# Perceiver block on one core: the first key group ahead of the queries, its loads first, GpSimd's fill of ones behind the norm

## The chip, the cores and the metric

One core of one Trainium2 chip. The metric is the device time of one execution in microseconds (us). The kernel before takes 1380.67 us, the median of three runs.

## The reference, cut to what matters

The program runs six residual layers over x (256 tokens, 256 features). The change lies in the first, a cross-attention of x to a context of 4096 tokens with 16 heads of 16 features:

```python
x = x + _L0_xattn_ref(_layernorm(x), ctx_1024, ctx_1024, Wq, bq, Wk, bk, ...)

Q = _linear(query, Wq, bq)      # 256 x 256, by heads
K = _linear(key, Wk, bk)        # 4096 x 256, by heads
V = _linear(value, Wv, bv)
scores = einsum('bhqd,bhkd->bhqk', Q, K) / sqrt(16)
# mean, maximum and variance of the softmax of scores give a temperature t for each head
attn = softmax(qk / (2 t))
out = _linear(attn @ V, Wo, bo)
```

The other five layers (linear attention, a block with 32 experts, a second cross-attention, multi-query attention, a mixture of 8 experts) are the same before and after.

## The kernel before, in words

The layer is `cross0`. It has several blocks, one after the other, and at the end of each block all engines meet at a barrier. The change touches only the first block, which computes the queries and the keys and splits both into three bfloat16 parts each (value, rest, rest of the rest), so that later float32 score products can be made from bfloat16 matmuls.

*VectorE* takes the layer norm of x (`layer_norm`, L118 to L129: statistics, `_rstd` at L124, a root on ScalarE, then xn at L128) and signals `xn_ready`. It then waits for the query matmuls, adds the bias (L342), signals `q_read`, splits the queries (L345 to L348), signals `q_split`, and sums them (L350). Then come the eight key groups, three instructions each (L355, L358, L360, the last signals `split_done`).

*TensorE* transposes xn (L158), multiplies it by wq (L291), and then makes eight key groups (L304). A group is one quarter of the context (1024 tokens, `ctxT`) by one half of the features: groups 0 to 3 are the four quarters with the first half, 4 to 7 the same with the second half. Four PSUM buffers hold the groups in turn. The transposes use buffer 0, the query product buffer 1, and group n uses buffer (n + 2) mod 4.

*ScalarE* takes the root, copies the transposed xn to SBUF (`xnT`, L318) and evacuates each group twice, as float32 (`whole`, L327) and as the first bfloat16 part (`parts`, L329). `whole` has two buffers, `parts` four. So group n waits for the split of group n - 2, and from group 4 on for the store of group n - 4:

```python
act.wait_ge(s["projected"], n + 1)
if n >= 2:
    act.wait_ge(s["split_done"], n - 1)
if n >= 4:
    act.wait_ge(stored[n % 4], 16 * (n // 4))
```

*SyncE* issues every DMA, in the order of the code. These are x, the identity, wq, bq, wk, the key bias `bcol`, and the four quarters of the context (L246 to L253). Then it waits for `q_split`, stores the three query parts (L257), waits for their landing, reads them back in another layout in six DMAs (L115), loads eight pieces of later weights (L263 to L268), and only then takes up the key groups: it waits for `split_done` of group n and stores its parts (L273). After group 3 it waits for all four stores and loads the keys of head 0 and 1 (L106), then stores groups 4 to 7.

*GpSimd* fills three rows of `k96` with ones (L311).

The next block (scores, from L450) starts at the barrier.

## Time and profile before

| | us |
|---|---|
| median of 3 runs | 1380.67 |
| lowest and highest run | 1380.11, 1383.14 |
| the profiled execution, its own time | 1385.94 |
| its span in the profile | 1384.2 |
| end of the first block's last split in that span | 49.33 |

The span is cut off a little at both ends of the execution, so it is 1.7 us shorter than the execution's own time. Times in the rows are in microseconds from the span's start. PE is TensorE, PEld its weight loads, DVE VectorE, ACT ScalarE, POOL GpSimd, SPq the queue of DMA issues on SyncE. A float32 matmul leaves two records in the trace, so four key matmuls of a half group (two blocks of 512 columns, two halves of the contraction) leave eight. Matmul records overlap; the rate is read from how many fall in a stretch, not from the length of one. What stands behind "<-" in brackets is what ended the idle time, as inferred by the view.

### The profile page before, as it was taken

What the parts mean: (1) busy time and instruction counts of PE and PEld (TensorE: products, weight loads), DVE (VectorE), ACT (ScalarE), POOL (GpSimd) and SP (SyncE); (2) the same over time, 40 slices, a digit from 0 to 9 for tenths busy, and PEclk for the clock granted to TensorE, in tenths of its full rate; (3) what the DMA queues carried; (4) which work ended last, traced back from release to release, by engine and by line L of the source; (5) the groups of instructions that cost most, each with busy time, mean ns of one, the idle gap of its engine ahead of it and who ended that gap; (6) DMA issues with size and microseconds to landing.
All of it is one profiled execution on the core that took longest, in us unless ns stands there. A gap on an engine that the chain in (4) does not pass through costs nothing. (4 is left out here: it accounts for less than half of the span.)

```text
span 1384.2 us, 25745 instructions
## 1 busy us (share of the span) xinstructions
PE 1129.8 (82%) x8423; PEld 694.0 (50%) x8423; DVE 816.0 (59%) x1508; ACT 899.7 (65%) x1208; POOL 630.7 (46%) x293
## 2 busy tenths in 40 slices
PE   7687877858999958979987788888888888857798
PEld 3343443433443436668872444454444444434687
DVE  6688888871111175552225787888887787735312
ACT  3599999967989724523322788888888888535110
POOL 2277777750000005000001899999999999800000
PEclk9799999988999968989995899999999999968899
DMA  7875445537555061004457899999999999524140
GB/s 253 249 220 129 119 118 134 125 91 149 106 118 99 0 208 64 1 31 152 152 214 247 309 324 313 312 327 331 323 316 325 313 330 324 189 70 168 45 138 8
DMA packets 97048, 257.51 MB, mean 186 GB/s; under 512 B 11193, under 2 KB 41305, under 8 KB 85466
## 3 DMA queue, kind: packets, MB, share of 16 engines
q1 hardware_dynamic: 96992, 256.79, 59.6%
q8 instruction: 32, 0.52, 0.2%
q14 instruction: 24, 0.20, 0.0%
HBM read 165.31 MB, written 91.92 MB: 186 GB/s over the span
## 5 line engine op out<-in xcount | busy, mean ns | idle before, releaser
L1916 POOL TENSOR_TENSOR xb_row<-xb_row,w_mask 128x1024 f32<-128x1024 f32 x128 | 419.4, 3293 | 246.3 <-DVE xb_row L1946 246.0
L1946 DVE TENSOR_TENSOR xb_row<-xb_cont_ps,xb_row 128x1024 f32<-128x1024 f32 x128 | 156.7, 1224 | 89.6 <-PE xb_cont_ps L1747 86.6
L554 DVE TENSOR_REDUCE xa_stats<-xa_b_ps 128x1 f32<-128x1024 f32 x128 | 155.7, 1219 | 33.4 <-PE xa_b_ps L470 32.8
L1784 PE MATMUL xb_turn_ps<-_ident,xb_row 128*128 128x128 f32 x1024 | 142.5, 284 | 38.8 <-ACT xb_row L1869 29.0
L1957 DVE CUSTOM_DVE_ANT_0 xb_row<-xb_row,xb_minus 128x1024 f32<-128x1024 f32 x128 | 165.5, 1293 | 0.0
L1784 PEld LDWEIGHTS xb_turn_ps<-_ident,xb_row 128*128 128x128 f32 x1024 | 113.6, 144 | 95.9 <-issue 61.2
L1747 PE MATMUL xb_cont_ps<-xb_kk,xb_qq 32*128 32x512 f32 x528 | 157.1, 673 | 2.4 <-DVE xb_row L1946 1.3
L1875 ACT COPY xb_turned<-xb_turn_ps 128x1024 f32<-128x1024 f32 x128 | 129.6, 1012 | 41.1 <-PE xb_turn_ps L1784 40.6
L1869 ACT ACTIVATE xb_row<-xb_row,xb_ntop 128x2048 f32<-128x2048 f32 x64 | 128.2, 2003 | 42.2 <-DVE xb_ntop L1963 42.2
L864 ACT ACTIVATE xa_probs<-xa_psT,xa_t_now 128x1024 f32<-128x1024 f32 x128 | 141.2, 1114 | 20.6 <-PE xa_psT L823 20.4
L1747 PE MATMUL xb_rel_ps<-xb_kk,xb_qq 32*128 32x512 f32 x496 | 145.9, 666 | 5.2 <-ACT xb_out L1864 4.0
L522 ACT ACTIVATE xa_exps<-xa_b_ps,xa_stats 128x1024 f32<-128x1024 f32 x128 | 141.2, 1108 | 13.5 <-DVE xa_stats L554 13.4
L1864 ACT COPY xb_out<-xb_rel_ps 128x1024 f32<-128x1024 f32 x124 | 124.8, 1006 | 29.8 <-PE xb_rel_ps L1747 16.1
L629 POOL TENSOR_TENSOR xa_rest<-xa_exps 128x1024 f32<-128x1024 f32 x48 | 90.9, 1894 | 99.9 <-ACT xa_exps L522 99.9
L1797 PE MATMUL xb_sum_ps<-xb_turned,xb_vhead 128*17 128x128 f32 x2048 | 82.5, 280 | 33.3 <-ACT xb_turned L1875 33.0
L1404 POOL TENSOR_TENSOR b_tc<-b_raw,w_waves 128x512 f32<-128x512 f32 x4 | 5.1, 1269 | 227.5 <-ACT b_raw L1390 227.5
L470 PE MATMUL xa_b_ps<-xa_k,xa_q 96*128 96x512 bf16 x256 | 71.0, 390 | 27.9 <-ACT xa_exps L522 17.3
L532 ACT ACTIVATE xa_squares<-xa_exps 128x1024 f32<-128x1024 f32 x80 | 84.2, 1053 | 0.5
L491 PE MATMUL xa_b_ps<-xa_wv,xa_ctxT 128*128 x512 | 67.2, 286 | 18.1 <-ACT xa_exps L522 18.1
L796 PE MATMUL xa_sums<-xa_probs,xa_vhead 128*17 128x256 f32 x1024 | 80.8, 389 | 0.2 <-ACT xa_probs L864 0.2
L491 PEld LDWEIGHTS xa_b_ps<-xa_wv,xa_ctxT 128*128 128x128 f32 x512 | 61.7, 196 | 33.1 <-ACT xa_exps L522 29.6
L1797 PEld LDWEIGHTS xb_sum_ps<-xb_turned,xb_vhead 128*17 128x17 f32 x2048 | 45.5, 98 | 63.4 <-ACT xb_turned L1875 51.9
(364 smaller groups left out, 1824.4 us busy)
## 6 DMA issues: line engine op xcount, KB each, us to landing
xb_row<-rel_scores SPq DMA_DIRECT2D x128, 512.0 KB, 5.9
rel_scores<-xb_out SPq DMA_DIRECT2D x32, 1024.5 KB, 5.7
rel_scores<-xb_out SPq DMA_DIRECT2D x32, 1024.0 KB, 5.3
b_e_w<-in_L_ffn_e_w SPq DMA_DIRECT2D x32, 513.0 KB, 3.5
w_w<-in_L_ffn_w SPq DMA_DIRECT2D x24, 512.0 KB, 4.6
xa_k<-first_parts SPq DMA_DIRECT2D x24, 384.0 KB, 5.1
value_rows<-xa_values SPq DMA_DIRECT2D x16, 544.0 KB, 6.1
xb_kk<-key_blocks SPq DMA_DIRECT2D x17, 512.0 KB, 7.8
```

The costliest lines, as they stand in the source:

```text
L491: mm = nc.tensor.matmul(out[:, n * P:(n + 1) * P], ctxT[:, k, at:at + P], wv[:, bass.ds(it, 1), k, :], start=(k == 0), stop=(k == KC - 1))
L522: nc.scalar.activation(exps[:, u % 4], ps[:, slot % 4], ACT.Exp, scale=-1.0, bias=stats[:, c % 2, 0, u:u + 1], accum_out=stats[:, c % 2, 1 ...
L554: nc.vector.tensor_reduce(stats[:, c % 2, 0, u:u + 1], ps[:, slot % 4], AX, ALU.min).then_inc(s["min_ready"], 1)
L864: nc.scalar.activation(probs[:, g % 4].rearrange("p c n -> p (c n)"), ps[:, g % 2], ACT.Exp, scale=t_now[:, b:b + 1]).then_inc(probs_ready, 1)
L1747: mm = nc.tensor.matmul(out[:, k * BANK:(k + 1) * BANK], qq[rows, b, kind, t * P:(t + 1) * P], kk[rows, b, half], start=True, stop=True)
L1784: mm = nc.tensor.transpose(turn_ps[:, k * P:(k + 1) * P], row[:, u, at:at + P], f.ident[:])
L1797: mm = nc.tensor.matmul(sum_ps[at:at + DV, 0:P], vhead[:, b, half * NCH // 2 + part * CPS + k, :], turned[:, part, k, :], start=(part == 0 ...
L1869: nc.scalar.activation(row[:, u], row[:, u], ACT.Exp, bias=ntop[:, u:u + 1]).then_inc(s["exp_done"], 1)
L1875: nc.scalar.copy(turned[:, part].rearrange("p k n -> p (k n)"), turn_ps[:]).then_inc(turned_sb[part], 1)
L1916: nc.gpsimd.tensor_tensor(row[:, u, at:at + SUB], row[:, u, at:at + SUB], mask[:, t, half * HALF + at:half * HALF + at + SUB], ALU.mult).t ...
L1946: nc.vector.tensor_tensor(row[:, u, at:at + SUB], cont_ps[:], row[:, u, at:at + SUB], ALU.add).then_inc(s["cont_out"], 1)
L1957: nc.vector.tensor_tensor_reduce(out=row[:, u, at:at + SUB], in0=row[:, u, at:at + SUB], in1=minus[:, t, half * HALF + at:half * HALF + at ...
```

## The change

Four edits, all in the first block:

1. SyncE issues wk third and the first quarter of the context fourth. bcol, wq and bq come behind them, ahead of the second quarter.
2. TensorE makes key group 0 first, then the transposes, group 1, the query matmuls, and groups 2 to 7. It waits for `q_read` ahead of group 3 instead of group 2, since the query product and group 3 share PSUM buffer 1.
3. ScalarE evacuates group 0 before it copies xnT. VectorE splits group 0 (`split_keys(0)`) before the queries (`split_queries`). SyncE's code behind the loads stays as it is.
4. GpSimd waits for `xn_ready` before it fills the ones.

```diff
--- before.py
+++ after.py
@@ -245,11 +245,12 @@
             def _(sp):
                 sp.dma_start(f.x[:], i["x"].rearrange("b (t p) d -> p (b t) d", p=P)).then_inc(s["x_loaded"], 16)
                 sp.dma_start(f.ident[:], i["c_ident"]).then_inc(s["x_loaded"], 16)
-                sp.dma_start(wq[:], rows_of(i["L0_xattn_Wq"])).then_inc(s["q_w_loaded"], 16)
-                sp.dma_start(bq[:], i["L0_xattn_bq"]).then_inc(s["q_w_loaded"], 16)
                 sp.dma_start(wk[:, 0], rows_of(i["L0_xattn_Wk"])).then_inc(s["k_w_loaded"], 16)
-                sp.dma_start(bcol[:, 0], i["L0_xattn_bk"]).then_inc(s["k_w_loaded"], 16)
                 for g in range(NQU):
+                    if g == 1:
+                        sp.dma_start(bcol[:, 0], i["L0_xattn_bk"]).then_inc(s["k_w_loaded"], 16)
+                        sp.dma_start(wq[:], rows_of(i["L0_xattn_Wq"])).then_inc(s["q_w_loaded"], 16)
+                        sp.dma_start(bq[:], i["L0_xattn_bq"]).then_inc(s["q_w_loaded"], 16)
                     sp.dma_start(ctxT[:, :, g * QUARTER:(g + 1) * QUARTER],
                                  rows_of(i["ctx_1024"])[:, :, g * QUARTER:(g + 1) * QUARTER]).then_inc(ctx_loaded[g], 16)
                 sp.wait_ge(s["q_split"], 1)
@@ -280,21 +281,10 @@
 
             @block.tensor
             def _(pe):
-                pe.wait_ge(s["x_loaded"], 32)
-                pe.wait_ge(s["xn_ready"], 1)
-                flat = ps[:, 0, 0:KC * S].rearrange("p (c n) -> p c n", c=KC)
-                transpose_tokens(nc, flat, xn, f.ident[:]).then_inc(s["xnT_mm"], 1)
-                pe.wait_ge(s["q_w_loaded"], 32)
-                pe.wait_ge(s["xnT_sb"], 1)
-                for m in range(KC):
-                    for c in range(KC):
-                        mm = nc.tensor.matmul(ps[:, 1, m * S:(m + 1) * S], wq[:, c, m * P:(m + 1) * P], xnT[:, c, :],
-                                              start=(c == 0), stop=(c == KC - 1))
-                mm.then_inc(s["q_mm"], 1)
-                pe.wait_ge(s["k_w_loaded"], 32)
-                for n, (g, t) in enumerate(key_groups):
+                def group(n):
+                    g, t = key_groups[n]
                     pe.wait_ge(ctx_loaded[g], 16)
-                    if n == 2:
+                    if n == 3:
                         pe.wait_ge(s["q_read"], 1)
                     if n >= 4:
                         pe.wait_ge(s["evacuated"], n - 3)
@@ -306,18 +296,38 @@
                                                   start=(c == 0), stop=(c == KC - 1))
                     mm.then_inc(s["projected"], 1)
 
+                pe.wait_ge(s["k_w_loaded"], 16)
+                group(0)
+                pe.wait_ge(s["x_loaded"], 32)
+                pe.wait_ge(s["xn_ready"], 1)
+                flat = ps[:, 0, 0:KC * S].rearrange("p (c n) -> p c n", c=KC)
+                transpose_tokens(nc, flat, xn, f.ident[:]).then_inc(s["xnT_mm"], 1)
+                group(1)
+                pe.wait_ge(s["q_w_loaded"], 32)
+                pe.wait_ge(s["xnT_sb"], 1)
+                for m in range(KC):
+                    for c in range(KC):
+                        mm = nc.tensor.matmul(ps[:, 1, m * S:(m + 1) * S], wq[:, c, m * P:(m + 1) * P], xnT[:, c, :],
+                                              start=(c == 0), stop=(c == KC - 1))
+                mm.then_inc(s["q_mm"], 1)
+                for n in range(2, len(key_groups)):
+                    group(n)
+
             @block.gpsimd
             def _(pool):
+                pool.wait_ge(s["xn_ready"], 1)
                 nc.gpsimd.memset(k96[ROWS:MAXROWS], 1.0).then_inc(s["ones_set"], 1)
                 pool.wait_ge(s["ones_set"], 1)
 
             @block.scalar
             def _(act):
                 take_root(f, act, s["var_ready"], s["root_ready"])
-                act.wait_ge(s["xnT_mm"], 1)
-                nc.scalar.copy(xnT[:], ps[:, 0, 0:KC * S].rearrange("p (c n) -> p c n", c=KC)).then_inc(s["xnT_sb"], 1)
                 act.wait_ge(s["k_w_loaded"], 32)
                 for n, (g, t) in enumerate(key_groups):
+                    if n == 1:
+                        act.wait_ge(s["xnT_mm"], 1)
+                        nc.scalar.copy(xnT[:], ps[:, 0, 0:KC * S].rearrange("p (c n) -> p c n", c=KC)
+                                       ).then_inc(s["xnT_sb"], 1)
                     act.wait_ge(s["projected"], n + 1)
                     if n >= 2:
                         act.wait_ge(s["split_done"], n - 1)
@@ -336,19 +346,7 @@
                 dve.wait_ge(s["x_loaded"], 32)
                 layer_norm(f, dve, step, xn, f.x, 1e-5, s["var_ready"], s["root_ready"])
                 dve.sem_inc(s["xn_ready"], 1)
-                dve.wait_ge(s["q_w_loaded"], 32)
-                dve.wait_ge(s["q_mm"], 1)
-                for m in range(KC):
-                    step(nc.vector.tensor_scalar(q[:, m], ps[:, 1, m * S:(m + 1) * S], bq[:, m:m + 1], -DK ** -0.5,
-                                                 ALU.add, ALU.mult))
-                dve.sem_inc(s["q_read"], 1)
-                step(nc.vector.tensor_copy(qparts[:, 0], q[:]))
-                step(nc.vector.tensor_tensor(qrest[:], q[:], qparts[:, 0], ALU.subtract))
-                step(nc.vector.tensor_copy(qparts[:, 1], qrest[:]))
-                step(nc.vector.tensor_tensor(qparts[:, 2], qrest[:], qparts[:, 1], ALU.subtract))
-                dve.sem_inc(s["q_split"], 1)
-                step(nc.vector.tensor_reduce(q_sums[:], q[:], AX, ALU.add))
-                for n in range(len(key_groups)):
+                def split_keys(n):
                     dve.wait_ge(s["evacuated"], n + 1)
                     if n >= 1:
                         dve.wait_ge(s["split_done"], n)
@@ -359,6 +357,25 @@
                     dve.wait_ge(s["second_done"], n + 1)
                     nc.vector.tensor_tensor(parts[:, n % 4, 2], rest[:], parts[:, n % 4, 1], ALU.subtract
                                             ).then_inc(s["split_done"], 1)
+
+                def split_queries():
+                    dve.wait_ge(s["q_w_loaded"], 32)
+                    dve.wait_ge(s["q_mm"], 1)
+                    for m in range(KC):
+                        step(nc.vector.tensor_scalar(q[:, m], ps[:, 1, m * S:(m + 1) * S], bq[:, m:m + 1], -DK ** -0.5,
+                                                     ALU.add, ALU.mult))
+                    dve.sem_inc(s["q_read"], 1)
+                    step(nc.vector.tensor_copy(qparts[:, 0], q[:]))
+                    step(nc.vector.tensor_tensor(qrest[:], q[:], qparts[:, 0], ALU.subtract))
+                    step(nc.vector.tensor_copy(qparts[:, 1], qrest[:]))
+                    step(nc.vector.tensor_tensor(qparts[:, 2], qrest[:], qparts[:, 1], ALU.subtract))
+                    dve.sem_inc(s["q_split"], 1)
+                    step(nc.vector.tensor_reduce(q_sums[:], q[:], AX, ALU.add))
+
+                split_keys(0)
+                split_queries()
+                for n in range(1, len(key_groups)):
+                    split_keys(n)
```

TensorE at the start of the block. Before (xa_a_ps is PSUM, in brackets the semaphores waited for; loaded0 and loaded1 are the quarters of the context):

```order
L158 MATMUL xa_a_ps<-_ident,xa_xn 128x128 [waits xa_a_xn_ready,xa_a_x_loaded]
L158 MATMUL xa_a_ps<-_ident,xa_xn 128x128 x3
L291 MATMUL xa_a_ps<-xa_xnT,xa_wq 128x256 [waits xa_a_xnT_sb,xa_a_q_w_loaded]
L291 MATMUL xa_a_ps<-xa_xnT,xa_wq 128x256 x3
L304 MATMUL xa_a_ps<-xa_ctxT,xa_wk 128x512 [waits xa_a_ctx_loaded0,xa_a_k_w_loaded]
L304 MATMUL xa_a_ps<-xa_ctxT,xa_wk 128x512 x3
L304 MATMUL xa_a_ps<-xa_ctxT,xa_wk 128x512 [waits xa_a_ctx_loaded1]
```

And with the change:

```order
L294 MATMUL xa_a_ps<-xa_ctxT,xa_wk 128x512 [waits xa_a_ctx_loaded0,xa_a_k_w_loaded]
L294 MATMUL xa_a_ps<-xa_ctxT,xa_wk 128x512 x3
L158 MATMUL xa_a_ps<-_ident,xa_xn 128x128 [waits xa_a_xn_ready,xa_a_x_loaded]
L158 MATMUL xa_a_ps<-_ident,xa_xn 128x128 x3
L294 MATMUL xa_a_ps<-xa_ctxT,xa_wk 128x512 [waits xa_a_ctx_loaded1]
L294 MATMUL xa_a_ps<-xa_ctxT,xa_wk 128x512 x3
L310 MATMUL xa_a_ps<-xa_xnT,xa_wq 128x256 [waits xa_a_xnT_sb,xa_a_q_w_loaded]
L310 MATMUL xa_a_ps<-xa_xnT,xa_wq 128x256 x3
```

The transposes now stand behind four matmuls of 512 columns, and the query matmuls behind four more.

VectorE from the end of the norm. Before:

```order
L128 TENSOR_SCALAR xa_xn<-_x,_mv,_rstd 128x256 [waits xa_a_dve_steps] x2
L342 TENSOR_SCALAR xa_q<-xa_a_ps,xa_bq 128x256 [waits xa_a_dve_steps,xa_a_q_mm,xa_a_q_w_loaded]
L342 TENSOR_SCALAR xa_q<-xa_a_ps,xa_bq 128x256 [waits xa_a_dve_steps]
L345 CAST xa_qparts<-xa_q 128x512 [waits xa_a_dve_steps]
L346 TENSOR_TENSOR xa_qrest<-xa_q,xa_qparts 128x512 [waits xa_a_dve_steps]
L347 CAST xa_qparts<-xa_qrest 128x512 [waits xa_a_dve_steps]
L348 TENSOR_TENSOR xa_qparts<-xa_qrest,xa_qparts 128x512 [waits xa_a_dve_steps]
L350 TENSOR_REDUCE xa_q_sums<-xa_q 128x2 [waits xa_a_dve_steps]
L355 TENSOR_TENSOR xa_rest<-xa_whole,xa_parts 128x1024 [waits xa_a_evacuated,xa_a_dve_steps]
L358 CAST xa_parts<-xa_rest 128x1024 [waits xa_a_rest_done]
L360 TENSOR_TENSOR xa_parts<-xa_rest,xa_parts 128x1024 [waits xa_a_second_done]
```

With the change:

```order
L128 TENSOR_SCALAR xa_xn<-_x,_mv,_rstd 128x256 [waits xa_a_dve_steps] x2
L353 TENSOR_TENSOR xa_rest<-xa_whole,xa_parts 128x1024 [waits xa_a_dve_steps,xa_a_evacuated]
L356 CAST xa_parts<-xa_rest 128x1024 [waits xa_a_rest_done]
L358 TENSOR_TENSOR xa_parts<-xa_rest,xa_parts 128x1024 [waits xa_a_second_done]
L365 TENSOR_SCALAR xa_q<-xa_a_ps,xa_bq 128x256 [waits xa_a_q_mm,xa_a_q_w_loaded]
L365 TENSOR_SCALAR xa_q<-xa_a_ps,xa_bq 128x256 [waits xa_a_dve_steps]
L368 CAST xa_qparts<-xa_q 128x512 [waits xa_a_dve_steps]
L369 TENSOR_TENSOR xa_qrest<-xa_q,xa_qparts 128x512 [waits xa_a_dve_steps]
L370 CAST xa_qparts<-xa_qrest 128x512 [waits xa_a_dve_steps]
L371 TENSOR_TENSOR xa_qparts<-xa_qrest,xa_qparts 128x512 [waits xa_a_dve_steps]
L373 TENSOR_REDUCE xa_q_sums<-xa_q 128x2 [waits xa_a_dve_steps]
L353 TENSOR_TENSOR xa_rest<-xa_whole,xa_parts 128x1024 [waits xa_a_split_done,xa_a_evacuated,xa_a_dve_steps]
```

The three instructions of the first key group have moved ahead of the seven of the queries.

SyncE at the start of the block. Before:

```order
L246 DMA _x<-in_x 128x2x256
L247 DMA _ident<-in_c_ident 128x128
L248 DMA xa_wq<-in_L_xattn_Wq 128x2x256
L249 DMA xa_bq<-in_L_xattn_bq 128x2
L250 DMA xa_wk<-in_L_xattn_Wk 128x2x256
L251 DMA xa_bcol<-in_L_xattn_bk 128x2
L253 DMA xa_ctxT<-in_ctx 128x2x1024 x4
```

With the change:

```order
L246 DMA _x<-in_x 128x2x256
L247 DMA _ident<-in_c_ident 128x128
L248 DMA xa_wk<-in_L_xattn_Wk 128x2x256
L254 DMA xa_ctxT<-in_ctx 128x2x1024
L251 DMA xa_bcol<-in_L_xattn_bk 128x2
L252 DMA xa_wq<-in_L_xattn_Wq 128x2x256
L253 DMA xa_bq<-in_L_xattn_bq 128x2
L254 DMA xa_ctxT<-in_ctx 128x2x1024 x3
```

The first quarter moved from the seventh to the fourth place. Behind the loads the queue is the same, with its wait for `q_split` ahead of everything else.

## Rows read from the trace of the kernel before

**Rows 1.** The page's first line.
```profile
span 1384.2 us, 25745 instructions
```

**Rows 2.** Timeline, SyncE's queue, 0 to 50: start, time of issue, instruction.
```profile
0.76 0.44 SPq L246 DMA_DIRECT2D _x<-in_x  x1
...
2.23 0.47 SPq L249 DMA_DIRECT2D xa_bq<-in_L_xattn_bq  x1
...
3.72 1.97 SPq L253 DMA_DIRECT2D xa_ctxT<-in_ctx  x4
...
18.39 1.41 SPq L257 DMA_DIRECT2D query_parts<-xa_qparts  x3
...
21.28 3.94 SPq L115 DMA_DIRECT2D xa_q<-query_parts  x6
...
29.27 5.04 SPq L273 DMA_DIRECT2D first_parts<-xa_parts  x4
...
39.89 3.75 SPq L106 DMA_DIRECT2D xa_k<-first_parts  x6
```

**Rows 3.** DMA view, issues at 3.7, 4.2, 29.2: last number is issue to landing.
```profile
xa_ctxT<-in_ctx SPq DMA_DIRECT2D x1, 1024.0 KB, 7.0
...
xa_ctxT<-in_ctx SPq DMA_DIRECT2D x1, 1024.0 KB, 9.1
...
first_parts<-xa_parts SPq DMA_DIRECT2D x1, 768.0 KB, 4.5
```

**Rows 4.** Timeline, TensorE, 9 to 42, with idle time before and its releaser.
```profile
9.23 1.09 PE L158 MATMUL xa_a_ps<-_ident,xa_xn 128*128 128x128 f32 x4 [9.23 <-DVEq L338]
...
11.09 3.60 PE L291 MATMUL xa_a_ps<-xa_xnT,xa_wq 128*128 128x256 f32 x8 [0.77 <-ACT xa_xnT L318]
...
14.53 27.63 PE L304 MATMUL xa_a_ps<-xa_ctxT,xa_wk 128*128 128x512 f32 x64
```

**Rows 5.** Timeline of the norm on GpSimd and VectorE; then line 124, min/median/max.
```profile
0.75 6.92 POOL L311 MEMSET xa_k<- 3x8192 bf16 x1 [0.29 <-POOLq L2704]
...
5.27 2.43 DVE L124 TENSOR_SCALAR _rstd<-_mv 128x2 f32<-128x2 f32 x1
...
8.17 0.86 DVE L128 TENSOR_SCALAR xa_xn<-_x,_mv,_rstd 128x256 f32<-128x256 f32 x2
...
L124 DVE TENSOR_SCALAR _rstd<-_mv x4: 168/168/2432, 5.3 to 1286.6; 128x2 f32<-128x2 f32 x4
```

**Rows 6.** Timeline, VectorE and ScalarE, 14 to 24.
```profile
14.81 1.00 DVE L342 TENSOR_SCALAR xa_q<-xa_a_ps,xa_bq 128x256 f32<-128x256 f32 x2 [5.78 <-PE xa_a_ps L291]
...
18.23 1.11 ACT L327 ACTIVATE xa_whole<-xa_a_ps,xa_bcol 128x1024 f32<-128x1024 f32 x1 [7.28 <-PE xa_a_ps L304]
...
18.46 0.69 DVE L350 TENSOR_REDUCE xa_q_sums<-xa_q 128x2 f32<-128x512 f32 x1 [0.15 <-DVE xa_qparts L348]
...
19.33 1.10 ACT L329 ACTIVATE xa_parts<-xa_a_ps,xa_bcol 128x1024 bf16<-128x1024 f32 x1
...
20.54 1.22 DVE L355 TENSOR_TENSOR xa_rest<-xa_whole,xa_parts 128x1024 f32<-128x1024 f32 x1 [1.40 <-ACT xa_parts L329]
...
22.53 1.22 DVE L360 TENSOR_TENSOR xa_parts<-xa_rest,xa_parts 128x1024 bf16<-128x1024 f32 x1
```

**Rows 7.** Timeline, VectorE and ScalarE, 29 to 51.
```profile
29.26 1.23 DVE L360 TENSOR_TENSOR xa_parts<-xa_rest,xa_parts 128x1024 bf16<-128x1024 f32 x1
...
32.69 1.23 DVE L360 TENSOR_TENSOR xa_parts<-xa_rest,xa_parts 128x1024 bf16<-128x1024 f32 x1
...
33.92 1.11 ACT L327 ACTIVATE xa_whole<-xa_a_ps,xa_bcol 128x1024 f32<-128x1024 f32 x1 [3.25 <-DVE xa_parts L360]
...
36.17 1.23 DVE L355 TENSOR_TENSOR xa_rest<-xa_whole,xa_parts 128x1024 f32<-128x1024 f32 x1 [2.25 <-ACT xa_parts L329]
...
48.10 1.23 DVE L360 TENSOR_TENSOR xa_parts<-xa_rest,xa_parts 128x1024 bf16<-128x1024 f32 x1
50.37 0.17 DVE L547 MEMSET xa_values<- 128x128 f32 x1 [1.04 <-PEq L236]
```

## Prediction

> **What bounds the opening now.** The change touches only the first block of the first layer, which ends at a barrier of all engines. I therefore read the span [rows 1], then SyncE's queue, the DMA landings, and the three compute engines up to the barrier.
>
> SyncE issues everything in one order [rows 2]. It issues loads until 5.7 us, then sits until the queries are split (18.39), stores their parts, waits for the landing, reads them back from 21.28, issues eight weight loads, and only at 29.27 comes to the stores of the key parts. From the wait for the queries to the first key store is 29.27 - 18.39 = 10.88 us, none of it waiting for a key group.
>
> The first quarter of the context lands at 3.72 + 7.0 = 10.7, the second at 4.2 + 9.1 = 13.3, and the first key store 29.27 + 4.5 = 33.8 [rows 3].
>
> TensorE starts at 9.23 and runs without a gap from 11.09 to 42.2 [rows 4]. The 64 records of the eight key groups follow each other every 27.63/64 = 0.43 us, so a group (8 records, 512 columns) takes 3.44. The eight query records have 256 columns and are also (14.53 - 11.09)/8 = 0.43 apart: half the rate per column. So TensorE worked at the lower of its two levels (1.2 GHz) from 9.23 until about 14.2 and at 2.4 GHz after, some 5.0 us from its first instruction.
>
> VectorE makes xn by 9.03 [rows 5]. One of its steps, of 128x2 elements, took 2.43 us where its like takes 0.168; it ended at 7.70, GpSimd's fill of ones at 7.67. That is the stall that the move of the fill removes. Query work runs from 14.81 to 19.15, ScalarE takes 19.33 + 1.10 - 18.23 = 2.2 to evacuate a group, VectorE 22.53 + 1.22 - 20.54 = 3.21 to split one [rows 6].
>
> **The wait that sets the end is the fifth group's** [rows 7]. Its evacuation starts at 33.92 though TensorE finished it at 14.53 + 5 x 3.44 = 31.7. The view names VectorE's split that ended at 33.92, but by the code group 4 needs three splits, and the third ended at 29.26 + 1.23 = 30.49. What is left is the store of group 0, whose buffer group 4 overwrites: it landed at 33.8. From there nothing is idle for long: VectorE begins that split at 36.17, four splits take (49.33 - 36.17)/4 = 3.29 each, the block ends at 49.33, and the next begins at 50.37. So the path is: query split, 10.88 us of SyncE, 4.5 of landing, then 15.5 us to the last split. Whatever moves the query split moves the end by as much; the splits in between have slack.
>
> **The change, part by part.**
>
> *Loads.* Context quarter 0 is issued in the slot of the old fourth load, at 2.23 instead of 3.72 [rows 2]. If it again takes 7.0, it lands at 9.2. Bounds: 10.7 if the start of the queue sets it (no gain). For the other end, x's load is issued at 0.76 and its work starts at once; at the pace of the later quarters (13.3 - 10.7 = 2.6 us per 1024 KB) the 1600 KB issued up to and with quarter 0 need 4.1 us, and with some 2 us for the first of it to arrive that gives 6.9. I take 9.2, since 7.0 is that very transfer. Quarter 1 keeps the same bytes ahead of it and lands at 13.3 as before.
>
> The Trainium skill, DMA: Bandwidth & Descriptors, section Anatomy of one DMA, fits a transfer (on GpSimd's path) as about 2.0 us and its bytes over 436 GB/s. By that the queue up to quarter 0 would land at 6.6 and quarter 1 at 9.5, against this trace's 10.7 where the same rule gives 7.2; the sum would be +3.7 us instead of what follows, and rival B has this case from rows.
>
> *The norm.* Without the stall xn is ready about 2.26 us earlier, at 6.8. This gains nothing: TensorE now takes key group 0 first, and that waits for quarter 0 until 9.2. The fill runs from 6.8 to 13.8 (6.92 us), while VectorE waits until after 17; cost nothing. If group 0 were as early as 6.9, VectorE's first cast would still come after 14.
>
> The Trainium skill, SBUF — State Buffer, section SBUF: two separate sides, calls the port pair of VectorE and GpSimd an exclusive lock that the loser waits out entirely; the 2.43 us step agrees. By that rule alone the sum would be -2.26, were the norm still what TensorE waits for.
>
> *TensorE.* Start 9.3, as before, but with 8 records of 512 columns. At the lower level one takes 0.86 (twice 0.43). If the level again rises 5.0 us after the start, 5.8 records are done by then and 2.2 go at 0.43: group 0 ends at 9.3 + 5.0 + 0.94 = 15.2. Ends: 12.7 were it all at 2.4 GHz, 16.2 were it all at 1.2. Then four transposes (half of 1.09, 0.5), group 1 (3.44, its data are there), and the query matmuls at full level, 8 x 0.215 = 1.7: the queries are ready at 20.9. ScalarE evacuates group 0 until 17.5 and copies xnT (0.59) until 18.1, before TensorE wants it at 19.2.
>
> *VectorE.* It splits group 0 from 17.6 to 20.8, about when the query result is ready, and starts on the queries at 20.9 + 0.28 = 21.2 (the trace has 0.28 from the next TensorE instruction, 14.53, to 14.81). Their split is then released 18.39 - 14.81 = 3.58 later, at 24.8, against 18.39: **+6.4 us**.
>
> *SyncE.* What stood behind the query wait stands there still. Group 0's parts are ready at 20.8, but the store is issued at 24.8 + 10.88 = 35.7 and lands at 40.2. Splits 1 to 3 run from 25.5 to 35.4, ready in time; VectorE then idles some 7 us instead of the 2.2 of before. The key loads of head 0 and 1 (39.89 before, behind the landing of all four stores) move by the same 6.4: the four stores left back to back before as well, one landing per 2 us.
>
> *Sum.* End of the block: 40.2 + 2.2 + 0.1 + 4 x 3.29, or by difference 49.33 + 6.4 = 55.7. After the barrier everything is the same program; TensorE has again idled for long before it (it still ends its eighth group near 42), so its level there is the same. No later slack takes the shift up, since all engines start at the barrier. The profiled execution took 1385.94 (span 1384.2), 5.3 above the median of 1380.67; it would become 1392.3, and the median 1380.67 + 6.4 = **1387.1**, +0.46%. A measurement of this kernel tells 0.2%, 2.8 us, from no change.
>
> **Rivals.**
>
> *B, the early part goes quicker.* Quarter 0 lands at 6.9, or TensorE is at 2.4 GHz for most of group 0. For it: 1024 KB in 7.0 us is slow beside the 2.6 of the next quarters. Against: the same trace, the same queue. Started at 7.0 and at the lower level until 12.0, group 0 ends at 12.9; group 1 still waits for 13.3, ends at 16.8, queries at 18.5, VectorE at 18.8: 4.0 instead of 6.4, so 1384.7. With quarter 1 early too it would be some +1.5 to +3.7, down to 1382.2.
>
> *C, quarter 0 is not early, or the lower level stays longer.* Landing at 10.7 and group 0 entirely at 0.86: it ends at 17.6, +2.4 on the forecast, 1389.5.
>
> *D, the other side: the store is not the gate.* If ScalarE's wait at 33.92 was really for VectorE, as the view names it, no SyncE store holds a buffer up, and only VectorE's work counts: queries done at 21.2 + 4.34 = 25.5, seven splits of 3.29, end 48.6 instead of 49.33: -0.8, 1379.9; with B's earlier queries -3.2, 1377.5. It decides as soon as the first store lands before VectorE has done split 3 (35.4), that is, 4.8 us earlier than computed. For it: one group's split (3.2 us) is indeed taken into time in which VectorE was idle. Against: the count in the code, and the 33.8 of the landing beside 33.92.
>
> *E, the change does not reach the end:* some wait behind the barrier (the landing of the last stores, 10 us behind) absorbs the shift, and the time stays at 1380.7. Against: those stores shift too.
>
> **How the numbers follow.** Forecast 0.62, B 0.16, C 0.10, D 0.07, E 0.05. B to C span 1384.7 to 1389.5; with the runs' own spread (about 1 us below and above) the range is 1383.4 to 1390.0, which leaves D, E and the extreme of B outside. D's lower half (0.03) is faster by over 0.2%; the rest of D, E and the extreme of B are within 0.2%: 0.10; slower 0.87.
>
> **What would show it.** In the changed profile: the first key matmul near 9.3 and its last near 15; query split stores from SyncE near 24.8; the first store of key parts near 35.7, and ScalarE idle before the fifth evacuation until about 40; VectorE's 128x2 step at 0.17 instead of 2.43; the last split ending near 55.7 and the next block at 56.8. Wrong if the fifth evacuation starts before its store has landed, if query stores leave before 21, or if the last split ends before 50.

## The result and the profile after

The changed kernel is slower. Its four runs have a median of 1392.47 us (1390.09 to 1395.22), the kernel before 1380.79 (1380.11 to 1383.14); the ratio of the two kernels' runs is 1.0058 with a 95% interval of 1.0034 to 1.0082, so +8.0 us with +4.7 to +11.3. Repeated later with 12 runs against 32 (e1 below), the ratio is 1.0043 (1.0027 to 1.0060), +5.9 us. The forecast of +6.4 lies in both intervals; the plain median of the first four runs, 1392.5, is above the range's 1390.0.

| profiled execution | before | after |
|---|---|---|
| its own time | 1385.94 | 1390.09 |
| span | 1384.2 | 1388.3 |
| TensorE's first matmul | 9.23 | 8.71 |
| query stores issued | 18.39 | 24.03 |
| first key store issued | 29.27 | 34.92 |
| fifth evacuation starts | 33.92 | 40.03 |
| next block's first instruction on VectorE | 50.37 | 56.47 |

Timeline of the changed kernel from the norm to the next block, all engines (start, duration, engine and line, instruction, in brackets the idle time before it and what ended it):

```profile
5.19 0.17 DVE L124 TENSOR_SCALAR _rstd<-_mv 128x2 f32<-128x2 f32 x1
...
5.83 0.86 DVE L128 TENSOR_SCALAR xa_xn<-_x,_mv,_rstd 128x256 f32<-128x256 f32 x2
6.80 6.92 POOL L319 MEMSET xa_k<- 3x8192 bf16 x1 [6.34 <-DVEq L348]
8.71 6.02 PE L294 MATMUL xa_a_ps<-xa_ctxT,xa_wk 128*128 128x512 f32 x8 [8.71 <-DMA xa_bcol<-in_L_xattn_bk]
...
14.57 0.60 PE L158 MATMUL xa_a_ps<-_ident,xa_xn 128*128 128x128 f32 x4
...
17.08 1.23 DVE L353 TENSOR_TENSOR xa_rest<-xa_whole,xa_parts 128x1024 f32<-128x1024 f32 x1 [10.39 <-ACT xa_parts L339]
...
18.44 1.89 PE L310 MATMUL xa_a_ps<-xa_xnT,xa_wq 128*128 128x256 f32 x8
...
20.45 1.00 DVE L365 TENSOR_SCALAR xa_q<-xa_a_ps,xa_bq 128x256 f32<-128x256 f32 x2 [0.16 <-PE xa_a_ps L310]
...
24.03 1.42 SPq L258 DMA_DIRECT2D query_parts<-xa_qparts  x3
...
34.92 3.57 SPq L274 DMA_DIRECT2D first_parts<-xa_parts  x4
40.03 1.11 ACT L337 ACTIVATE xa_whole<-xa_a_ps,xa_bcol 128x1024 f32<-128x1024 f32 x1 [9.69 <-DMA first_parts<-xa_parts]
...
42.27 1.22 DVE L353 TENSOR_TENSOR xa_rest<-xa_whole,xa_parts 128x1024 f32<-128x1024 f32 x1 [7.61 <-ACT xa_parts L339]
...
54.21 1.23 DVE L358 TENSOR_TENSOR xa_parts<-xa_rest,xa_parts 128x1024 bf16<-128x1024 f32 x1
56.47 0.17 DVE L564 MEMSET xa_values<- 128x128 f32 x1 [1.04 <-PEq L236]
...
65.42 0.75 DVE L581 TENSOR_SCALAR xa_whole<-xa_b_ps,xa_bcol 128x512 f32<-128x512 f32 x1 [1.97 <-SPq L418]
```

What the reader is to see: the norm is faster (0.17 for the step that took 2.43 in [rows 5]) and nobody uses it, since TensorE works on key group 0 until the transposes start at 14.57. The query matmuls come at 18.4 and SyncE's query stores at 24.03. From there to the first key store are 10.89 us, as in [rows 2] (10.88). And the view now itself names the landing of a key store as what ended ScalarE's wait before the fifth evacuation (40.03), where it had named VectorE in [rows 7]. VectorE's fourth split had ended 5.4 us before that.

One label is not to be taken at its word. The view puts TensorE's start at 8.71 down to `bcol`. By the code TensorE waits for 16 of `k_w_loaded`, which wk alone gives (issued at 1.75, landed 3.6 later), and for quarter 0. In e1 it started at 8.24, after quarter 0 (2.23 + 5.9 = 8.1) and before `bcol` (2.74 + 5.6 = 8.3), so quarter 0 is what it waits for. A kernel to be copied should still give wk a semaphore of its own: two loads in flight count to this one, and a count of 16 does not say by itself which of them it came from.

The DMA view of the changed kernel, for the issues at 2.2 and 34.9 (last number: issue to landing):

```profile
xa_ctxT<-in_ctx SPq DMA_DIRECT2D x1, 1024.0 KB, 6.3
...
first_parts<-xa_parts SPq DMA_DIRECT2D x1, 768.0 KB, 5.0
```

Quarter 0 landed at 2.22 + 6.3 = 8.5; the store of group 0 at 34.92 + 5.0 = 39.9, just ahead of the 40.03.

The last line of the timeline is of a kind that the prediction did not look at. It is the first product that VectorE takes out in the next block. By the code it waits for a signal of SyncE, and SyncE gives it once all eight key stores have landed; SyncE's own next issue stands right behind that signal. Timeline, VectorE and SyncE, before and then with the change:

```profile
60.08 0.75 DVE L564 TENSOR_SCALAR xa_whole<-xa_b_ps,xa_bcol 128x512 f32<-128x512 f32 x1 [2.61 <-SPq L401]
60.22 1.58 SPq L405 DMA_DIRECT2D key_blocks<-in_ctx  x2
```

```profile
65.56 1.58 SPq L422 DMA_DIRECT2D key_blocks<-in_ctx  x2
```

In both, SyncE goes on 0.14 us behind the product's start. (In e1 the view puts the product's wait down to TensorE, but SyncE goes on 0.14 us behind it there too, at 64.84.) So the shift is 6.1 us at the barrier (56.47 - 50.37) and 5.3 us at this second place (65.42 - 60.08).

### The profile page after: what moved, and what is told of

It reads as the page before. It is cut to its first block and busy times, and to the rows that moved or that the text cites. A ratio compares the mean times of both kernels' runs of the same rounds, so it can differ in the third digit from the quotient of the medians.

```text
span 1388.3 us, 25744 instructions
## 1 busy us (share of the span) xinstructions
PE 1129.7 (81%) x8423; PEld 693.5 (50%) x8423; DVE 814.1 (59%) x1508; ACT 899.7 (65%) x1208; POOL 630.4 (45%) x293
## 5 line engine op out<-in xcount | busy, mean ns | idle before, releaser
L1801 PE MATMUL xb_turn_ps<-_ident,xb_row 128*128 128x128 f32 x1024 | 144.0, 286 | 38.8 <-ACT xb_row L1886 29.2
```

Source lines behind the costliest of these rows:

```text
L1801: mm = nc.tensor.transpose(turn_ps[:, k * P:(k + 1) * P], row[:, u, at:at + P], f.ident[:])
```

## The experiments

Two times are read from every profile: when VectorE begins the next block (the *barrier*), and when it takes out that block's first product (the *product*). Theory S is that of the prediction: the query split releases SyncE's queue, whose key stores gate the splits. Rival V: VectorE's own work is the gate. Theory P: a shift of the barrier costs again later, by where TensorE's low level falls. After e1 to e4 came theory G: there are two gates, the barrier and the product, and a shift of the barrier alone does not reach the end.

| kernel | barrier | product | ratio to before (95%) | us |
|---|---|---|---|---|
| before | 50.37 | 60.08 | 1 | |
| the change | 56.47 | 65.42 | 1.0058 (1.0034 to 1.0082) | +8.0 |
| e1 the change again | 56.05 | 64.70 | 1.0043 (1.0027 to 1.0060) | +5.9 |
| e2 delay only | 56.08 | 64.86 | 1.0029 (1.0008 to 1.0049) | +4.0 |
| e3 fill alone | 49.27 | 59.44 | 0.9996 (0.9977 to 1.0015) | -0.6 |
| e4 change, loads between stores | 52.96 | 64.98 | 1.0050 (1.0032 to 1.0067) | +6.9 |
| e5 change, first store early | 52.07 | 62.42 | 1.0016 (1.0000 to 1.0032) | +2.2 |
| e6 change, loads early | 52.76 | 61.52 | 1.0002 (0.9984 to 1.0020) | +0.3 |
| e7 before, fill and loads early | 48.00 | 57.37 | 0.9975 (0.9957 to 0.9992) | -3.5 |
| e8 before, head 1's keys later | 50.46 | 58.18 | 0.9976 (0.9957 to 0.9996) | -3.3 |
| e9 order alone | 58.24 | 67.13 | 1.0051 (1.0033 to 1.0068) | +7.0 |
| e10 opening loads alone | 50.51 | 59.77 | 0.9994 (0.9974 to 1.0014) | -0.8 |
| e11 before, fill, head 1's keys later | 48.30 | 55.46 | 0.9959 (0.9941 to 0.9978) | -5.7 |
| e12 before, all three | 48.14 | 54.42 | 0.9959 (0.9941 to 0.9976) | -5.7 |

The last column is the ratio less one, times the 1380.79 of before. Each ratio is to runs of before that were made along with that kernel's, and the two places are read from one profile of each, so a few tenths in them are not the edit's: the change and e1 are the same kernel and differ by 0.4 and 0.7.

One reading of the whole table: the shift of the product against before lies inside the interval of the total in every row. The shift of the barrier does not in e4 (+2.6 against +4.4 to +9.3), e8 (+0.1 against -5.9 to -0.6), e11 (-2.1 against -8.1 to -3.0) and e12 (-2.2 against -8.1 to -3.3).

**e1, the change again.** No edit.

> The changed kernel once more, for the size of the difference. Theory S (the path runs from the query split through SyncE's queue and the landing of group 0's store; the first block ends 6.1 us later and nothing else changes): ratio about 1.0044, +6 us; first block's last split ends near 55.4. Theory P (a shift of the barrier alone also moves where TensorE's low-clock stretches fall in the rest of the program, and that costs as much again): +10 to +12 us.

+5.9 us (+3.7 to +8.3): theory S's size, not P's. But one execution differs much from the next: these 12 runs lie between 1383.75 and 1395.21. The profile shows a part of what differs. The next two lines are the same instruction of VectorE, behind the end of the scores block, first in e1 and then in the first profile of the same kernel (before has it at 303.81):

```profile
307.56 0.28 DVE L707 TENSOR_SCALAR xa_w3b<-_ident,xa_w 64x128 f32<-64x128 f32 x1 [0.55 <-PEq L384]
```

```profile
310.12 0.28 DVE L707 TENSOR_SCALAR xa_w3b<-_ident,xa_w 64x128 f32<-64x128 f32 x1 [0.55 <-PEq L384]
```

The barriers of the two are 0.4 us apart, these rows 2.6. In between, TensorE's granted clock differs. A stretch by windows (us; busy of PE, PEld, DVE, ACT and POOL with counts; granted clock; DMA share; GB/s), again e1 and then the first profile:

```profile
240.00:260.00 20.00, 15.38 (x74) 8.29 (x73) 16.40 (x18) 19.53 (x34) 14.92 (x12) 1.00 0.55 129
```

```profile
240.00:260.00 20.00, 15.52 (x76) 8.80 (x75) 14.61 (x17) 17.98 (x32) 13.91 (x12) 0.91 0.43 107
```

Before has 0.91 there too. A mean of 0.91 over 20 us is, as an estimate, 3.6 us at 1.2 GHz (half the clock) in a stretch that is otherwise at 2.4; one execution has it and the next has not. From 66 to 90 us the two have 0.93 and 0.86. That these stretches make up the 2.2 us between the rows is likely and not shown; what makes the clock fall in one execution and not in the other stays open. So a single span (1388.3, 1382.0) says little about a change of 6 us, and the places in the first 66 us say much.

**e2, delay only.**

```diff
                 step(nc.vector.tensor_copy(qparts[:, 1], qrest[:]))
+                for _ in range(12):
+                    step(nc.vector.tensor_copy(qparts[:, 1], qrest[:]))
                 step(nc.vector.tensor_tensor(qparts[:, 2], qrest[:], qparts[:, 1], ALU.subtract))
```

> The kernel before, with 12 more casts of 128x512 (0.43 us each, 0.46 apart) on VectorE between the query split and its signal: 5.5 us of delay and no other part of the change. Theory S: SyncE's query stores leave at 18.4 + 5.5 = 23.9, the first key store at 34.8, the last split ends near 55, total +5.5 to +6.1, the same as the changed kernel within the noise. Rival V (VectorE's own work bounds the block, and the wait of the fifth evacuation is for VectorE's split, as the view names it): the seven splits behind the queries start 5 us later too, so it also gives +5, but ScalarE's wait before the fifth evacuation then ends with the fourth split and not with a landing. Theory P: total +10 to +12 us from the same 6 us at the barrier.

Query stores at 24.08, key store at 34.96, barrier 56.08, product 64.86: the changed kernel's opening, by a late query split and nothing else. The total, +4.0 (+1.1 to +6.8): the interval holds S's +5.5 and excludes P's +10. Timeline, VectorE and ScalarE:

```profile
36.81 1.23 DVE L362 TENSOR_TENSOR xa_parts<-xa_rest,xa_parts 128x1024 bf16<-128x1024 f32 x1
...
39.63 1.11 ACT L327 ACTIVATE xa_whole<-xa_a_ps,xa_bcol 128x1024 f32<-128x1024 f32 x1 [5.92 <-DMA first_parts<-xa_parts]
```

VectorE ended the fourth split at 38.04, and the fifth evacuation started 1.6 us later, at the landing. Rival V falls.

**e3, fill alone.**

```diff
             def _(pool):
+                pool.wait_ge(s["xn_ready"], 1)
                 nc.gpsimd.memset(k96[ROWS:MAXROWS], 1.0).then_inc(s["ones_set"], 1)
```

> The kernel before with only GpSimd's fill behind the norm. In the old order the norm is what TensorE waits for, so the 2.43 us step falls to 0.17 and everything behind comes 2.26 us earlier: TensorE starts at 7.0, query stores leave at 16.1, the fifth evacuation starts at 31.7, the last split ends at 47.1; total -2.3 us (0.9984). Rival: the fill, now at 6.8 to 13.7, stops a VectorE cast of the query split (which would start near 13.7), and some of it is given back: -1.5 to -2.2. Rival L: the key group 0 waits for its quarter (10.7), which is hidden behind the queries: no effect on the end.

The norm's step took 0.17 and TensorE started at 6.92, 2.31 earlier. But only 1.1 of it reached the barrier and 0.6 the product; the total, -0.6 (-3.2 to +2.1), can't be told from no change. Timeline, SyncE's queue:

```profile
16.23 1.41 SPq L257 DMA_DIRECT2D query_parts<-xa_qparts  x3
19.71 3.94 SPq L115 DMA_DIRECT2D xa_q<-query_parts  x6
```

Between the two lie 3.48 us where [rows 2] have 2.89, and the store of group 0 took 5.0 to land instead of 4.5; that is where 1.1 of the expected 2.3 went. The query stores left while the context was still loading (its last quarter landed at 5.2 + 13.4 = 18.6), but that alone does not explain the loss. In e11 the same fill stands in the same opening, and the context landed at 18.1, again behind the query stores:

```profile
16.22 1.42 SPq L257 DMA_DIRECT2D query_parts<-xa_qparts  x3
19.21 3.94 SPq L115 DMA_DIRECT2D xa_q<-query_parts  x6
```

There the two are 2.99 apart, the store took 4.5, and 2.1 us reached the barrier. So in these two profiles the fill is worth 1.1 and 2.1 us at the barrier, and why e3's transfers were slower stays open. The rival (a stopped cast) did not show: the cast takes 0.43 as before.

**e4, the change with eight loads moved between the key stores.** SyncE's eight loads of later weights now follow the store of group 2:

```diff
+                    if n == 2:
+                        load_later()
```

> The changed kernel, with SyncE's eight loads of later weights (4.0 us of issue) moved from ahead of the key stores to behind the store of group 2. Theory S: the store of group 0 leaves 4.0 us earlier, at 30.9, lands near 35.5, the fifth evacuation starts then, the last split ends near 51.4, total -4.0 us against the changed kernel (+2 against the kernel before). Rival V: the splits are not held by stores, the block still ends near 55.4 and the total stays.

The barrier came 3.1 us earlier than in e1, the product did not (64.98 against 64.70), and the total did not move (+6.9 against +5.9) where -4.0 was expected. Timeline, SyncE and VectorE:

```profile
33.04 1.35 SPq L265 DMA_DIRECT2D xa_wk<-in_L_xattn_Wk  x1
34.43 1.29 SPq L265 DMA_DIRECT2D xa_wk<-in_L_xattn_Wp  x1
...
40.31 0.47 SPq L275 DMA_DIRECT2D first_parts<-xa_parts  x1
46.06 3.74 SPq L106 DMA_DIRECT2D xa_k<-first_parts  x6
...
64.98 0.75 DVE L584 TENSOR_SCALAR xa_whole<-xa_b_ps,xa_bcol 128x512 f32<-128x512 f32 x1 [5.05 <-SPq L421]
```

Behind three large stores one issue took 1.3 us instead of 0.45, the store of group 3 left only at 40.3, and the key loads at 46.06 (45.69 in e1). So the last stores landed when they did before, and VectorE idled 5.05 us for them. This is the run that parts barrier and product, and it made theory G.

**e5, the change with the store of group 0 ahead of the query wait.**

```diff
+                store_parts(0)
                 sp.wait_ge(s["q_split"], 1)
...
-                for n, (g, t) in enumerate(key_groups):
+                for n in range(1, len(key_groups)):
+                    store_parts(n)
```

> The changed kernel, with the store of group 0 moved ahead of SyncE's wait for the query split; stores 1 to 7 stay where they are. Theory S: group 0 is split at 20.3, its store leaves then and lands near 24, so the fifth evacuation no longer waits for it (it starts near 31.5) and the sixth waits for the store of group 1 (34.9 + 4.5 = 39.4) instead; the last split ends near 51.5. Theory G (two gates: the first product that VectorE takes out in the next block waits for the landing of all eight stores, which follow the key loads of heads 0 and 1 in one queue and land some 20 us after these are issued): the key loads come only one store, 2 us, earlier (43.7 instead of 45.7), so that product comes at about 62.7 to 63.4 instead of 64.7 to 65.4, and of the 3.9 us at the barrier only 2 reach it.

Barrier 52.07 (4.0 earlier than e1), product 62.42 (2.3 earlier), as G said. Timeline, VectorE:

```profile
62.42 0.75 DVE L586 TENSOR_SCALAR xa_whole<-xa_b_ps,xa_bcol 128x512 f32<-128x512 f32 x1 [3.63 <-SPq L423]
```

The total went from +5.9 to +2.2, that is -3.7, where 2 were expected; the two intervals are some 2 us wide to either side and don't tell 2 from 4.

**e6, the change with the eight loads behind the context.** The same eight loads, moved up to stand ahead of SyncE's `wait_ge(s["q_split"], 1)`.

> The changed kernel, with SyncE's eight loads of later weights issued right behind the context, ahead of the wait for the query split, while the queue has nothing to issue. Theory S: the first key store leaves at 30.9, lands near 35.4, the last split ends near 51. Theory G: the key loads come at about 41 instead of 45.7 and the last store lands near 61, so both gates come 4 to 4.7 us earlier and the total is 4 us below the changed kernel, where moving the loads between the stores moved only the barrier and not the total.

Key store at 31.62, key loads at 42.32, barrier at 52.76 and product at 61.52 (3.3 and 3.2 earlier than e1, where 4 to 4.7 were expected), total +0.3 (-2.2 to +2.8) against e1's +5.9. In this execution quarter 0 landed at 9.9 and TensorE started at 10.08 instead of 8.24, which put the query stores 0.7 later than in e1; the run does not tell whether the eight loads did that. The same move of work as in e4, to a place where it delays no key load, and now the product and the total follow.

**e7, the old order with fill and early loads.** The kernel before with e3's edit and e6's.

> The kernel before, in its old order, with the fill behind the norm and the eight loads issued right behind the context: the two parts that should help without what delays the queries. Query stores leave near 16.2, the first key store as soon as the fourth split lets it, near 23 to 24, and lands by 28.5; no evacuation waits for a store. TensorE's groups bound the block: it starts them at 12.3 and ends the eighth at 39.9, the last split ends near 45.3 (49.3 before). Key loads near 36.5 (39.9 before), last landing near 56.7 (60.0). Theory G: total -3.3 to -4 us against the kernel before (0.997). Theory S alone says the same of the barrier.

Total -3.5, as expected, but by another way: barrier 48.0 rather than about 46.3, product 57.37 rather than 56.7. Timeline, SyncE's queue:

```profile
16.79 3.01 SPq L265 DMA_DIRECT2D query_parts<-xa_qparts  x3
22.80 3.94 SPq L115 DMA_DIRECT2D xa_q<-query_parts  x6
```

The read back came 6.0 us behind the start of the query stores instead of 2.9 (e12, with the same early loads, has 6.0 too), so of the 4 us of issue taken off the path 3.1 were given back. The first key store left at 26.79, not at 23 to 24, and landed at about 31.5, where the fifth evacuation started (31.56): against the expectation it still waited for a store.

**e8, head 1's keys later.** Only head 0's keys are loaded in the first block; head 1's at the start of the next:

```diff
-                        for h in range(2):
-                            load_first_keys(f, sp, k96[0:ROWS, h], h, k_loaded[h])
+                        load_first_keys(f, sp, k96[0:ROWS, 0], 0, k_loaded[0])
...
                 sp.sem_inc(k_free, 2)
+                load_first_keys(f, sp, k96[0:ROWS, 1], 1, k_loaded[1])
```

> The kernel before, with head 1's key loads issued at the start of the next block, behind the stores of groups 4 to 7 and not ahead of them. It measures the second gate alone. Theory G: the last split and the barrier stay (49.3, 50.4), the last store lands near 53 to 55 instead of 60, VectorE's first product in the next block starts near 57.5 and not at 60.1, and the total falls by up to 2.6 us (0.998), unless head 1 then waits for its keys. Theory S alone (the barrier is all that counts): the product's start and the total stay.

Barrier 50.46, unchanged; product 58.18, 1.9 earlier; total -3.3 (-5.9 to -0.6). The last landing was no longer what the product waited for: SyncE went on at 56.63, 1.5 us ahead of the product, and VectorE came to it from a reduction, without idle time. Timeline, SyncE and VectorE:

```profile
56.63 1.59 SPq L405 DMA_DIRECT2D key_blocks<-in_ctx  x2
...
57.03 1.23 DVE L554 TENSOR_REDUCE xa_stats<-xa_b_ps 128x1 f32<-128x1024 f32 x1 [2.69 <-PE xa_b_ps L470]
58.18 0.74 DVE L564 TENSOR_SCALAR xa_whole<-xa_b_ps,xa_bcol 128x512 f32<-128x512 f32 x1
```

The second gate is real, in the kernel before too.

**e9, the order alone.** The changed kernel with the old order of loads and the fill at the start (and TensorE's first wait for 32 of `k_w_loaded`).

> The kernel before with only the new order of TensorE, ScalarE and VectorE (key group 0 first, group 1 ahead of the query matmuls); loads and fill as before. Theory S: the order is what costs, and the two other parts had hidden some of it. Quarter 0 lands at 10.7 and not at 8.5, so TensorE starts some 2.1 us later than in the changed kernel, the query stores leave near 25.6 to 26.5 (24.0 there, 18.4 before), the last split ends near 57 to 58, total +7 to +8 us (1.005 to 1.006). Rival: the order gives back a group's split early and the parts only cost together: total within 2 us of before.

Timeline, TensorE and SyncE:

```profile
11.08 5.88 PE L293 MATMUL xa_a_ps<-xa_ctxT,xa_wk 128*128 128x512 f32 x8 [11.08 <-DMA xa_ctxT<-in_ctx]
...
26.26 1.41 SPq L257 DMA_DIRECT2D query_parts<-xa_qparts  x3
```

Barrier +7.9, product +7.05, total +7.0 (+4.6 to +9.4). The order is the whole of the loss. The two other parts gave some 2.2 us of it back at the query stores and the barrier (24.06 and 56.05 in e1), since quarter 0 came earlier; in the totals 7.0 and 5.9 can't be told apart.

**e10, the opening loads alone.** The kernel before with only SyncE's new order of the opening loads.

> The kernel before with only the new order of the opening loads. Theory S: TensorE still waits for the norm until 9.0, so an earlier quarter 0 is not used; wq lands near 8.9 and is wanted at 11.1. Query stores leave at 18.4, the last split ends at 49.3, total 0. Rival: the query weights now come too late behind quarter 0 and hold the query matmuls, up to +1.

Query stores at 18.54, barrier at 50.51, product at 59.77, total -0.8 (-3.6 to +1.9): no change that can be told, as expected.

**e11 and e12, the best versions.** e11 is e3 and e8 together; e12 adds the early loads of e7.

> The kernel before in its old order, with the fill behind the norm and head 1's key loads at the start of the next block. Theory G: the fill alone moved the barrier by 1.1 us but the second gate by only 0.7; with the gate out of the way the barrier's gain is kept: barrier near 49.2, VectorE's first product in the next block near 56, total -3 to -4 us (0.9975).

> The kernel before in its old order, with the fill behind the norm, the eight later loads behind the context, and head 1's key loads at the start of the next block. Theory G: barrier near 48.0 as with the first two alone, last store landing no longer waited for, VectorE's first product in the next block near 55 (60.1 before), total -5 us against the kernel before (0.9965). Rival: head 1 then waits for its keys and gives a part of it back.

Both are 0.9959 of before, -5.7 us (e11 -8.1 to -3.0, e12 -8.1 to -3.3), a little more than the -3 to -4 and -5 that were expected. Against e8 the fill moved the barrier of e11 by 2.2 us and its product by 2.7: with the last landing out of the way, a gain at the barrier is kept. e12's product comes 1.0 us earlier than e11's, which the total does not show. Timeline of e12, VectorE, the product again without idle time:

```profile
54.42 0.74 DVE L565 TENSOR_SCALAR xa_whole<-xa_b_ps,xa_bcol 128x512 f32<-128x512 f32 x1
```

## Why the prediction was right, and where not

*The mechanism* was right and is shown: a delay of the query split alone (e2) makes the changed kernel's opening, the order alone (e9) makes its loss, and taking the store out of the way (e5, e6) takes most of it back. "Whatever moves the query split moves the end by as much" held in e2 (5.7 at the query stores, 5.7 at the barrier) and in e11 (2.2 and 2.1), but not in e3 (2.2 and 1.1).

*Quarter 0*: taken to land at 9.2, landed at 8.5 (6.3 us instead of 7.0), within the bounds of 6.9 to 10.7. The fit of the Trainium skill, DMA: Bandwidth & Descriptors, section Anatomy of one DMA, as the prediction worked it out, gave 6.6 (its terms add up to 6.5); the trace does not agree, and the measurement stands. *Group 0*: taken to end at 15.2; the transposes behind it started at 14.57. Its time is not fixed: from its start to the transposes it took 5.86 us here, 6.36 in e1 (8.24 to 14.60) and 4.99 in e5 (8.92 to 13.91). *The lower level*: the prediction inferred it from the spacing of matmuls. The weight loads of the changed kernel confirm the spacing (one every 0.86 us until 13.11, every 0.43 from 13.71), but the windows view prints a granted clock of 1.00 from 8.7 to 14.6, and for the kernel before from 9 on. So the doubled spacing is shown, and that it is the level of 1.2 GHz is an inference that no clock record here supports. *Query split*: 24.8, was 24.03; +5.6 instead of +6.4, almost all of it from the earlier start and the shorter group 0; the steps behind (transposes, group 1, query matmuls, 3.58 us of query work) fitted within 0.1 us each.

*The landing*: taken as 4.5 after issue, was 5.0 in the first profile, and the fifth evacuation came 5.1 behind the issue; this made the barrier +6.1 in spite of the +5.6. (In e1 the landing took 4.6, and the barrier is at +5.7.) The last split was to end at 55.7 and ended at 55.44. That the two misses nearly cancelled was luck.

*The range*: it was built on a spread of "about 1 us below and above". Twelve runs of the changed kernel lie 11 us apart, and 32 of before 10. That +6.4 fits so closely says little about errors of 1 us in its terms.

*What failed* is the step "no later slack takes the shift up, since all engines start at the barrier", and the answer to rival E, "those stores shift too". They do shift, but by the time of the key loads (+5.9 us, 39.89 to 45.75), not of the barrier. VectorE waits for them in the next block, before and after, and so a gain at the barrier was worth nothing while they landed as late (e4), and a gain at them was worth something with the barrier where it was (e8). For this change the two places moved by 6.1 and 5.3, so slack behind the barrier took up 0.8 and the sum was hardly touched; for e4, e8, e11 and e12 it decides. I read the waits only up to the barrier, where the row at 60.08 would have told.

*The norm and the fill*: in the changed kernel nothing waits for them, as said. The step of 128x2 elements fell from 2.43 to 0.17 us, which agrees with the exclusive lock of the Trainium skill, SBUF — State Buffer, section SBUF: two separate sides; in the old order the same edit starts TensorE 2.3 us earlier (e3). By that rule of the Trainium skill one would expect this as the gain; in e3 1.1 of it reached the barrier and 0.6 the product.

*The rivals*: B was right in its cause (quarter 0 earlier), by 0.7 us and not by 2.3, so its price was small. D, the other side, is refuted by the 40.03 of the changed kernel and the 39.63 of e2, both behind VectorE's split and at the landing. E exists in part: 0.8 of 6.1 us.

## What to carry to other kernels

When steps are reordered, ask first who waits for the step that becomes late, and on which in-order queue that wait stands: here three small query stores, 5.6 us late, held back every key store of the one DMA queue, while the group that was made early could not leave. Follow a wait one barrier further than the change: a block that begins with a wait for the landing of the last block's stores has its real start there. And move transfers to where the queue is idle and nothing that is waited for stands behind them: the same eight loads were worth nothing at the product between the stores (e4) and 3.2 us ahead of them (e6, where the total fell by 5.6, give or take 3.4).

## What the runs showed of the hardware that was not expected

The key loads are slow for what they occupy. Stretches of the kernel before by windows, while the six key loads are in the queue and while the stores behind them are:

```profile
45.00:50.00 5.00, 0.00 (x0) 0.00 (x0) 4.16 (x4) 0.00 (x0) 0.00 (x0) 0.51 0.97 164
50.00:55.00 5.00, 4.24 (x8) 1.78 (x9) 2.52 (x3) 1.74 (x2) 0.00 (x0) 0.50 1.05 350
```

The DMA engines are busy in both (0.97 and 1.05, as the view prints it), at 164 and at 350 GB/s. The four stores behind the six key loads land 9.7 to 11.9 us after their issue; in e8, behind three key loads, 6.7 to 7.7. That is what e8 gains. Why the key loads are slow was not tested; each writes 16, 32 or 48 partitions.

An issue on SyncE costs 0.43 to 0.47 us for the opening loads, 0.6 for the key loads, and 1.3 us behind three stores of 768 KB (e4) or behind the four quarters of the context (e6: 5.16 us for four loads of 128 KB). The first key group of the changed order takes 5.0 to 6.4 us in six profiles (starts from 8.24 to 11.08), where a later group takes 3.44.

The time of one kernel on one chip spread over 11 us in 12 runs, with the granted clock of one profile's stretch at 1.00 where another's has 0.91; with about 12 runs against 32, the interval still reaches 2.5 us to either side.
